# Latent attention in a six-layer decoder kernel: the causal mask added by VectorE in PSUM in place of TensorE's mask products

## The reference

```python
q = concat(q_nope, q_rope)            # 16 heads
k = concat(k_nope, k_rope)            # 4 key heads, each for 4 query heads
scores = einsum('bqhd,bkhd->bhqk', q, k) * scale
causal = tril(ones((s, s), dtype=bool))            # s = 256
scores = where(causal[None, None], scores, finfo(scores.dtype).min)
attn = softmax(scores, axis=-1)
out = einsum('bhqk,bkhd->bqhd', attn, v_p).reshape(b, s, H * FULL)
return out @ Wo
```

## Time and profile before

| what | us |
|---|---|
| median of 3 runs | 855.43 (853.38 to 862.85) |
| the profiled execution, device time | 851.29 |
| its span in the profile | 849.4 |
| PE busy | 717.7 (84%) |
| DVE busy | 441.4 (52%) |
| ACT busy | 397.4 (47%) |
| POOL busy | 203.4 (24%) |

### The profile page before, as it was taken

How to read it: one execution, slowest core, us unless ns; L and a number is a source line. 1 busy time by engine, 2 the same in 40 slices (tenths; PEclk the granted TensorE clock), 3 DMA queues, 4 the chain that set the end, 5 groups by cost and what they waited for, 6 DMA issues and landing times.

```text
span 849.4 us, 13794 instructions
## 1 busy us (share of the span) xinstructions
PE 717.7 (84%) x4888; PEld 577.3 (68%) x4893; DVE 441.4 (52%) x1040; ACT 397.4 (47%) x1091; POOL 203.4 (24%) x351
## 2 busy tenths in 40 slices
PE   6887889999999997587989999998776279999960
PEld 4665778989889885355878888887665236666640
DVE  2676764675865845785545454444247712222214
ACT  3987664475555643664656454554321022222212
POOL 2454300000100101362123232333103602222224
PEclk9998999999999999898989999999989579999995
DMA  8993002202203101401000000000290211111104
GB/s 316 368 317 74 2 1 78 78 1 79 78 1 117 39 1 62 186 1 54 22 1 1 1 2 1 1 2 1 88 431 20 75 38 44 44 50 43 43 31 148
DMA packets 32258, 62.48 MB, mean 74 GB/s; under 512 B 2724, under 2 KB 26984, under 8 KB 29896
## 3 DMA queue, kind: packets, MB, share of 16 engines
q1 hardware_dynamic: 30184, 56.48, 19.4%
q0 software_dynamic: 2016, 5.22, 1.8%
HBM read 46.24 MB, written 15.55 MB: 73 GB/s over the span
## 4 chain that ended last, share of the span: by engine, by line
PE 59%; DVE 14%; ACT 14%; POOL 5%; DMA 4%; issue 4%; SPq 0%; POOLq 0%; DVEq 0%; ACTq 0%
PE banks L1594 39%; PE bank L1594 20%; ACT arena L706 4%; DVE U_split L1119 3%; ACT arena L937 2%; ACT U_split L725 2%; POOL xs L620 2%; DMA arena<-in_w_qr 2%; POOL rstd L527 1%; DVE mx L1073 1%; POOL rstd L524 1%; DVE arena L1292 1%; DMA ys<-arena 1%; ACT arena L744 1%; DVE fh L1295 1%
## 5 line engine op out<-in xcount | busy, mean ns | idle before, releaser
L1594 PE MATMUL banks<-arena 128*128 (+4 forms) x816 | 189.4, 426 | 3.8 <-DVE arena L1067 2.3
L1594 PEld LDWEIGHTS banks<-arena 128*128 128x128 f32 (+2 forms) x816 | 111.1, 184 | 49.8 <-issue 38.0
L1594 PE MATMUL bank<-U_split 128*128 128x256 f32 (+1 forms) x864 | 115.9, 290 | 16.1 <-DVE U_split L1119 14.6
L1594 PEld LDWEIGHTS bank<-U_split 128*128 128x128 f32 x864 | 108.8, 194 | 20.4 <-issue 16.5
L1594 PE MATMUL banks<-U_split 128*128 128x256 f32 (+1 forms) x624 | 101.7, 313 | 1.4 <-DVE U_split L1192 1.4
L1594 PE MATMUL banks<-cst,arena 128*128 128x128 f32 (+1 forms) x594 | 84.2, 277 | 17.3 <-DMA arena<-xs 11.8
L1594 PEld LDWEIGHTS banks<-cst,arena 128*128 128x128 f32 (+1 forms) x594 | 69.9, 142 | 39.0 <-issue 25.3
L1594 PEld LDWEIGHTS banks<-U_split 128*128 128x128 f32 x624 | 86.2, 193 | 10.5 <-issue 5.0
L937 ACT ACTIVATE arena<-banks,dmx 128x128 f32<-128x128 f32 (+1 forms) x128 | 52.4, 418 | 76.0 <-DVE dmx L1393 76.0
L524 POOL TENSOR_SCALAR rstd<-mv 128x1 f32<-128x1 f32 x48 | 14.7, 307 | 304.4 <-DVE mv L1051 280.8
L595 POOL TENSOR_SCALAR arena<-arena,dri 128x128 f32<-128x128 f32 (+1 forms) x128 | 52.0, 425 | 140.8 <-DVE dri L1359 140.8
(11 more groups left out here) (213 smaller groups left out, 1198.7 us busy)
## 6 DMA issues: line engine op xcount, KB each, us to landing
arena<-in_w_exp SPq DMA_DIRECT2D x8, 1536.0 KB, 14.2
xs<-arena SPq DMA_DIRECT2D x8, 1032.0 KB, 14.2
arena<-in_ctxT SPq DMA_DIRECT2D x4, 1601.0 KB, 7.4
arena<-in_ctx SPq DMA_DIRECT2D x4, 1536.0 KB
arena<-in_w_f SPq DMA_DIRECT2D x3, 1024.0 KB, 12.6
arena<-xs SPq DMA_DIRECT2D x23, 129.0 KB, 2.1
...
```

The lines of the kernel that those rows point to most:

```text
L1594: return nc.tensor.matmul(o, w, x, start=start, stop=stop, **k)
```

## The change

The bias shrinks to the one diagonal block. PE's scores of a head are two products that each start and end their own part of the bank. DVE adds the bias, for both heads of a round, to blocks 0 and 2 of the bank in place (one instruction a head, the bias broadcast over the two blocks), and only then takes the maxima, each head's waiting for its add (new semaphore d_add). DVE's wait for the bias replaces PE's. Two semaphores of weight loads are merged into one, so that POOL's rotation of the query weights also waits for w_oh. `before16` in the router is read from the one block.

```diff
--- before.py
+++ after.py
@@ -126,7 +126,7 @@
 def causal_bias():
 
     d = np.where(np.arange(P)[:, None] >= np.arange(P)[None, :], 0, NEG)
-    return np.concatenate([d, np.zeros((P, P)), d], 1).astype(np.float32)
+    return d.astype(np.float32)
 
 
 def build(nc, d, xs, ys, out):
@@ -179,7 +179,7 @@
         parity = cst[:, C_PAR:C_PAR + 2]
         tri = cst[:, C_TRI:C_TRI + NE * NE].rearrange("p (a b) -> p a b", a=NE)
         ident16 = sb("ident16", [P, P], BF16)
-        cbias = sb("cbias", [P, 3 * P], BF16)
+        cbias = sb("cbias", [P, P], BF16)
         ones = sb("ones", [P, P])
         magic = sb("magic", [P, 1])
         mhalf = sb("mhalf", [P, 1])
@@ -345,7 +345,7 @@
         eri = sb("eri", [P, TPB, KT * HT])
 
 
-        names = """ld_x ld_q0 ld_k0 ld_v0 ld_rows ld_x01 ld_ctxT ld_ctxR ld_ffn ld_lat ld_cbias ld_wq ld_wo ld_out
+        names = """ld_x ld_q0 ld_k0 ld_v0 ld_rows ld_x01 ld_ctxT ld_ctxR ld_ffn ld_lat ld_cbias ld_wqo ld_out
             const_set ln_var ln_rstd ln_done xT_raw xT_done
             a_q a_k a_v a_q_sb a_k_sb a_v_sb a_vmix a_s a_add a_max a_exp a_rinv a_norm
             a_pt a_pt_act a_pt_dve a_o a_o_sb a_y a_y_sb ld_rest
@@ -353,7 +353,7 @@
             x_k x_neg x_exp x_kf x_kf_hi x_kf_lo x_m1 x_m1_sb x_m1T x_m1T_sb x_kv x_kvbd
             w_abs w_sum w_scale w_round w_tern
             f_sc f_fac f_round f_q f_qT f_qT_sb f_gu f_sig f_h f_hsc f_hround f_hq f_hqT f_hqT_sb f_y
-            d_w d_w_sb d_c d_c_sb d_k d_k_sb d_rot d_q d_q_sb d_s d_max d_exp d_rinv d_norm
+            d_w d_w_sb d_c d_c_sb d_k d_k_sb d_rot d_q d_q_sb d_s d_add d_max d_exp d_rinv d_norm
             d_t d_t_sb d_o d_o_sb d_o_lo d_y
             e_g e_sig e_q e_exp e_qf e_nd e_av e_avT e_at e_y
             ld_zero ld_exp r_set r_log r_act r_exp r_v r_kept r_count r_rows m_ids r_scat r_table
@@ -453,11 +453,11 @@
                 load_ctxR(b)
 
             sp.wait_ge(G["w_tern"], 3)
-            load(w_oh, d["w_oh"], "ld_wo")
+            load(w_oh, d["w_oh"], "ld_wqo")
 
             sp.wait_ge(G["b_o"], 2 * B)
-            load(w_qT, d["w_qT"], "ld_wq")
-            load(w_qr, d["w_qr"], "ld_wq")
+            load(w_qT, d["w_qT"], "ld_wqo")
+            load(w_qr, d["w_qr"], "ld_wqo")
 
             for n in range(NE):
                 if n == 0:
@@ -579,7 +579,7 @@
 
             rots = [0]
             pool.wait_ge(G["ld_lat"], 96)
-            pool.wait_ge(G["ld_wq"], 32)
+            pool.wait_ge(G["ld_wqo"], 48)
             for n in range(NT):
                 if n < 2:
                     rotate(w_ki[:, :, LAT:P], w_kr[:, :, :], LAT, KV1, n)
@@ -1369,6 +1369,7 @@
             NP = B * PAIRS
             d_split_w(0)
             d_split_w(1)
+            dve.wait_ge(G["ld_cbias"], 16)
             d_query(0)
             for p in range(NP + 1):
                 b, q = divmod(p, PAIRS)
@@ -1388,6 +1389,10 @@
                 if p < NP:
                     for h in (2 * p, 2 * p + 1):
                         dve.wait_ge(G["d_s"], h + 1)
+                        own = PS[2 + h % 2][:, 0:4 * P].rearrange("p (c d k) -> p c d k", c=2, d=2)[:, :, 0, :]
+                        v.tensor_tensor(own, own, cbias[:, :].unsqueeze(1).broadcast_to([P, TPB, P]), ALU.add).then_inc(G["d_add"], 1)
+                    for h in (2 * p, 2 * p + 1):
+                        dve.wait_ge(G["d_add"], h + 1)
                         bank = PS[2 + h % 2]
                         v.tensor_reduce(dmx[:, h % 8, 0:1], bank[:, 0:P], AX, ALU.max, negate=True).then_inc(G["d_max"], 1)
                         v.tensor_reduce(dmx[:, h % 8, 1:2], bank[:, P:3 * P], AX, ALU.max, negate=True).then_inc(G["d_max"], 1)
@@ -1463,7 +1468,7 @@
 
 
             dve.wait_ge(G["ld_cbias"], 16)
-            v.tensor_scalar(before16, cbias[:, 0:P], 0.0, None, ALU.is_lt).then_inc(G["r_set"], 1)
+            v.tensor_scalar(before16, cbias[:, :], 0.0, None, ALU.is_lt).then_inc(G["r_set"], 1)
             v.tensor_copy(ones16, ones[:, :]).then_inc(G["r_set"], 1)
 
             def e_ln(b):
@@ -1993,8 +1998,7 @@
 
                 if t == 0:
                     pe.wait_ge(G["ld_lat"], 96)
-                    pe.wait_ge(G["ld_wq"], 32)
-                    pe.wait_ge(G["ld_wo"], 16)
+                    pe.wait_ge(G["ld_wqo"], 48)
                     pe.wait_ge(G["ln_var"], 2 * NT)
                 else:
                     pe.wait_ge(G["d_w_sb"], 2 * t)
@@ -2081,9 +2085,8 @@
                     pe.wait_ge(G["d_exp"], 2 * (h - 2) + 2)
                 q = qe[:, p % 3, h % 2, :]
                 k = kg[:, b % 2, g, :]
-                mm(o[:, 0:3 * P], ident16[:, :], cbias[:, :], stop=False)
-                mm(o[:, 0:P], q[:, 0:P], k[:, 0:P], start=False, stop=False)
-                mm(o[:, P:3 * P], q[:, P:S], k, start=False, stop=True).then_inc(G["d_s"], 1)
+                mm(o[:, 0:P], q[:, 0:P], k[:, 0:P])
+                mm(o[:, P:3 * P], q[:, P:S], k).then_inc(G["d_s"], 1)
 
             def d_transpose(h):
                 pe.wait_ge(G["d_norm"], 2 * h + 2)
@@ -2122,7 +2125,6 @@
                                 [w[:, i, :] for w in (w_vo, w_vh)], start=i == 0, stop=i == PAIRS - 1)
                 ins.then_inc(G["d_y"], 1)
 
-            pe.wait_ge(G["ld_cbias"], 16)
             NP = B * PAIRS
             for p in range(NP + 4):
                 b, q = divmod(p, PAIRS)
```

## The result

| what | us |
|---|---|
| changed kernel, median of 4 runs | 872.01 (866.34 to 876.51) |
| kernel before, median of 4 runs on the same chip | 858.16 (853.38 to 862.85) |
| ratio | 1.0219, 95% interval 1.0166 to 1.0272 |
| predicted | 866 (856 to 876), slower by over 1% at 0.60 |
| profiled execution of the changed kernel | 876.51 (span 874.6) |

The change makes the kernel slower by 1.7 to 2.7% by the interval of the ratio; the quotient of the two medians is 1.016. The direction and the mechanism were as predicted and the time lies in the range, but the size was set too low: 866 against a median of 855.43 is 1.2%.

A forecast was written before the change was run, and what follows sets the result against it. The PE bounds many rounds (4.74 us), with a DVE-ACT loop only 0.36 us shorter bounding about ten. Loop and lag shifts of 12.0 us plus 1 for clock gave +13, put at 866 us, range 856 to 876.

The forecast's parts named there:

- The loop: DVE to ACT to DVE in each round of two heads: two adds lengthen it from 4.38 to 5.06 us.
- The PE's own round: PE's work for one pair of heads: without the two mask products it falls from 4.74 to 4.41 us.
- the added lag of 0.83: Scores' start to first exponential, 1.69 to 2.51 us: +0.83 in each round whose start is set by the PE.
- 0 to 5: First five steps between rounds, loop-bound while DVE splits weights: 5 x 0.68 = 3.4 us longer.
- 5 to 6: Step through the keys and second key product, ending in a PE start: +0.83 us.
- 14 to 20: PE-bound rounds: four longer loops, mostly taken back by the output products, 34.04 to 34.66 us, +0.6.
- the step 10 to 11: Loop-bound step before round 11's output products: its growth hides under them, adding nothing to the shift.
- the term for the clock: Round 13's key step: a PE gap 0.83 longer loses full clock, at better than even odds, +1 us.
- the step from the sum to the time: Whole kernel: +13 us on the profiled 851.3 gives 864.3, on the median 868.4; 866 was chosen.
- rival 2: PE-bound rounds: adds fit DVE's idle time, PE's gain of 6.6 us arrives, 849 us; chance 0.08.
- rival 3: Nearly even: adds cheap (0.2) or output products and key steps absorb more; +2 to +8, 857 to 863; chance 0.18.
- rival 4: PE waits in most rounds and its clock falls to half in four to eight more; 872 to 881 us; chance 0.12.

The follow-up runs named there:

- no_mask: The changed kernel without DVE's adds, so no causal mask is applied at all; ratio 0.9885 to the kernel before.
- before_again: The kernel before, unchanged, timed and profiled once more; 860.16 us, ratio 0.9999 to the kernel before.
- after_again: The changed kernel, unchanged, timed and profiled once more; 875.76 us, ratio 1.0189 to the kernel before.
- query_first: The changed kernel with DVE's query copy moved ahead of the low part of the output; ratio 1.0106 to the kernel before.
- hybrid: The kernel before with the query copy mostly ahead of the output's low part and DVE adding the mask only in rounds 14 to 20 and 22 to 28; ratio 0.9897.

## Why the prediction was right, and where its size was wrong

**The loop.** 5.06 predicted, 5.03 to 5.04 measured. The terms held one by one: an add 425 ns long, the next instruction 0.34 behind it (518.08 to 518.74 is 0.66 for two; I had 0.68), DVE's idle time unchanged before L1119. I had quoted the Trainium skill (VectorE: DVE Perf Modes, "The DRAIN you can't avoid") with half of what it says: that the next instruction waits until the pipe is empty, which gave 5.22. The same section adds that an instruction that is not held starts earlier, and by their spacing of 0.34 us the adds were of that kind. The PE's own round, 4.41, was measured as 4.39 by no_mask.

**The sum, step by step** (shift of the first maxima against the profile of before, ahead of which stands the added lag of 0.83 at round 0):

| rounds | predicted | measured |
|---|---|---|
| 0 to 5 | +3.4 | +3.28 |
| 5 to 6 | +0.83 | +0.19 |
| 6 to 7 | +0.3 | +0.29 |
| 7 to 10 | +2.04 | +1.96 |
| 12 to 13 | -0.33 | -0.33 |
| 13 to 14 | +0.83, +1 for the clock | +2.38 |
| 14 to 20 | +0.6 | +0.68 |
| 20 to 22 | -0.33 + 0.83 | -0.33 + 0.78 |
| 22 to 28 | +0.6 | +0.72 |
| 28 to 31 | +2.4 | +2.04 |
| 0 to 31 | | +12.44 |

With the 0.83 that is 13.3 against 13 predicted. Two entries need a word. 5 to 6: the lag there was longer in the kernel before, since the scores of round 6 ran at half clock (scores at 442.13, first maximum 443.75, 1.62 us), and 1.86 in the changed kernel at full clock (452.81 to 454.67); my 1.03 was the lag at full clock. From 10 to 12 another 0.8 came that I had at nothing: I had said that the growth of the step 10 to 11 hides under the output products, and it was carried on to round 12.

**What failed.** Two terms of the size, not the mechanism.

First, the term for the clock: "With the gap 0.83 longer I expect it in round 13 too, at better than even odds: +1." The profile of before had lost its clock in the step 21 to 22, and I took that to be the rule of the kernel. It was one of two profiles of it, and over the kernels with the short gap two steps of twelve, against fifteen of sixteen with the long one. By these counts the longer gap alone costs 2 x 1.6 x (15/16 - 2/12) = 2.5 us; between before_again and after_again the two steps grew by 2.41 and 2.39 us, which is 3.1 beyond the two lags of 0.83. The step 29 to 30 I had without any clock. Over all executions after_again stood 12.5 us longer at half clock, worth 5.1 us by the estimate above, where I had 1.

Second, the step from the sum to the time: "Total +13 us, on the profiled execution's 851.3: 864.3. Its time is 4.1 below the median of the runs shown, 855.4, which would give 868.4. I say 866." That is 10.6 us on the median for a sum of 13. The sum is a difference, and belongs on the median; 2.4 us were given away in that sentence.

Put together: I had 12.0 us of loop and lag, 1 of clock and -2.4 of base, 10.6 on the median. Measured were 13.9 and 15.4 as differences of medians (872.01 less 858.16, 875.76 less 860.38), and in the second comparison 15.6 as a difference of means, of which 10.5 are loop and lag and 5.1 clock. The two ratios, 1.022 and 1.019, stand for 16 to 19 us. For the first comparison the clocks of the kernel before are not on record, so what its ratio has beyond that stays open. I had also written that the time outside the stage would be unchanged. Between the first two profiles it was not: 7.45 us ahead of round 0, and 256.9 us behind round 31's first maximum in before against 262.2 in after. Yet it was 261.3 in before_again and 259.8 in after_again, with the same code, so I can't put the difference down to the change.

**The lag.** Predicted: 1.03 from the scores' start to the first maximum becoming 1.86: measured 1.86 at 452.81 to 454.67, and 3.39 from round 5's first exponential to the second key product in both kernels (434.04 to 437.43, 444.77 to 448.16), as the step over the keys was drawn. query_first and hybrid show it from the other side: the same adds cost nothing where a round's start doesn't hang on them.

**The rivals.** The PE's gain (rival 2) exists, 8.0 us in no_mask's stage with some 1.5 of clock in it, and doesn't arrive. It arrives in query_first's rounds at 4.44, which needs the copy moved, not a cheaper add. Nearly even (rival 3) is out: an add takes 0.34 and not 0.2, and the shift without the clock's part came to 10.5 of the 12 us, not to 2 to 8. The clock (rival 4) was underrated at 0.12. It didn't fall because the PE waits in most rounds, since PE-bound and loop-bound rounds alike stood at 1.00, but it cost some 5 us where I had 1, and the measured 872.01 lies at the lower end of that rival's range as it does at the upper end of my own. (That rival's 881 is its 13 us on 868; on the 866 of the forecast it would be 879.)
